# Pooling of the image tiles split between GpSimd and VectorE in a fused vision tower

## The chip, the cores and the metric

The kernel runs on one core of a Trainium2 chip. The metric is device time of one execution in microseconds; lower is better. The kernel before has a median of 2033.8 us over 3 runs (2013.52 to 2034.38).

## What is computed

The input is 64 images of 12 planes of 224 x 224 float32 (154 MB). The reference is a tower of three layers; cut to what matters here:

```python
# layer 1, for each image: sums over patches of 16 x 16 pixels, then a small product
pooled = x.reshape(B, 12, 14, 16, 14, 16).sum(axis=(3, 5))
h = einsum('bcij,ce->bije', pooled, channel_weights)      # 196 tokens of 192
# layer 2: h += softmax(Q K^T / sqrt(192)) V on the layernorm of h, one head
# layer 3 on the layernorm of h: a router takes the best 98 of 196 tokens for each of
#   4 experts (top_k of a softmax); fc1 with an MLP part (768) and q, k, v (12 heads of 16),
#   attention over 196 tokens, gelu, fc2, weighted by the gates, added to h
```

## The kernel before, in words

**Groups and bodies.** Images go in 8 groups of 8. While the third layer's attention and MLP of one group run, the pooling, the first attention and the routing of the next are done in between. The program is a prologue (pooling and routing of group 0 with nothing beside them, and pooling of the first half of group 1), a loop body that runs six times, a body behind it for the second last group, and a last body that has no next group. A body has 96 slots: 8 images by 12 heads. In each slot TensorE computes one head's scores twice (`peak`, whose row maxima VectorE takes, and `score`, whose exponentials ScalarE takes); the other work is placed at slot numbers. Behind the 96 slots the body has an opening, which computes the hidden layer of the next group.

**The order** on every engine is this one list, sorted by slot number; each engine walks through it and executes the entries that have a part for it, strictly in order. Engines wait for each other by semaphores alone. A slot number sets only what comes behind what; it is no time.

**Pooling.** A tile holds 8 planes: 112 partitions (8 planes x 14 rows of patches), each with 16 x 224 = 3584 floats, 1.6 MB. A group has 12 tiles, in 4 pairs of images (`m`) of 3 tiles (`t`). There are three tile buffers (`NX`). For a tile, in order: ScalarE's queue issues the load (`fetch`), VectorE sums the patches with seven `tensor_reduce`, each for two of the 14 patch columns (`pool`, L1211), GpSimd spreads the 14 sums over a masked square (`own_row`, L1457), TensorE adds the three tiles of a pair (`planes`, L734) and makes tokens of them (`tok`, L744). The semaphore `pooled` counts tiles that VectorE has summed; both `own_row` and the load of the tile three further on wait for it. In a loop body, tiles 6 to 11 of the next group are pooled from slot 0 on (`pace` 0.8: one `pool` every 0.8 slots), and tiles 0 to 5 of the group after it from slot 42 on (`pace` 1.25). The body behind the loop has the first six alone, the last body none.

**Routing** of the next group begins at slot 37 in a body: `norm1_scale` (VectorE sums, GpSimd raises to the power -0.5 in L1466, VectorE multiplies in L1243 and copies in L1247, TensorE transposes in L752), then 8 steps `first_max` and 8 steps `first_exp`, for each of which GpSimd makes a masked copy (`own_image`, L1486), then the gates (`gate_scale`, `gate_logits`, `gates`: two more powers on GpSimd, between them and behind them short VectorE instructions such as L1322 and L1328), then `choose`: 13 rounds on VectorE, each the eight largest of a row (L1342) and their replacement (L1347). Each round needs the one before. `chosen` (L834 on TensorE) waits for the last of them, `spread` (L1364, L1367) is behind it on VectorE, and the next group's `turn_u`, `project` and `hidden` on TensorE need `spread`.

**GpSimd** has, beside the masked copies, `own_row` and the powers, one addition per image to the result (`fc2`, L1494).

## Time and profile before

| | |
|---|---|
| runs | 2013.52, 2034.38, 2033.8 us; median 2033.8 |
| the profiled execution | 2031.33 us, its span 2029.5 us (1.8 us lie outside the span) |
| granted TensorE clock, mean | 0.861 of full speed |
| TensorE matmul busy | 1627.6 us, 80% |
| VectorE busy | 1226.3 us, 60% |
| ScalarE busy | 846.7 us, 42% |
| GpSimd busy | 248.4 us, 12% |

The page's line for an engine gives its busy time, the share of the span and the number of instructions. A group of instructions is one source line with one shape; "idle before" is how long the engine stood still just before them, and what it then waited for. TensorE is called PE, its weight loads PEld, VectorE DVE, ScalarE ACT, GpSimd POOL. Where a wait ends by "issue", the profile shows no releaser.

### The profile page before, as it was taken

The page shows a single profiled execution, that of the slowest core. Times are in us where ns is not written, and L with a number is a line of the kernel's source. Part 1 is how long each engine was busy: PE and PEld are TensorE (multiplying, and loading weights), DVE is VectorE, ACT ScalarE, POOL GpSimd, SP SyncE. Part 2 cuts the span into 40 slices and gives each one's busy share as a digit, 9 for nine tenths or more (in the row PEclk, how much of TensorE's full clock was granted, in tenths as well). Part 3 has the DMA queues.
Part 4 walks back from the last instruction along what each step waited for, and adds up shares of the span by engine and source line. Part 5 has one row for each costly group of instructions (what it writes and reads, how often), then busy time and mean ns, then how long its engine had stood idle before and what let it go on. Part 6 is the DMA issues. An engine that isn't in the chain of part 4 may idle for free.

```text
span 2029.5 us, 39123 instructions
## 1 busy us (share of the span) xinstructions
PE 1627.6 (80%) x12434; PEld 1306.0 (64%) x12434; DVE 1226.3 (60%) x2822; ACT 846.7 (42%) x1934; POOL 248.4 (12%) x318
## 2 busy tenths in 40 slices
PE   5116388968998788969799688987889698988998
PEld 2004366757676677758577576766667576767786
DVE  2465577673776557773776647664676747553453
ACT  1001154434444344435444344433544354544653
POOL 2002001110012001110011100210011100210000
PEclk8557599978799788978899789987899788998899
DMA  2993456433764437424655337534464335211220
GB/s 70 220 248 103 116 119 151 105 101 70 170 133 107 101 89 180 102 71 101 152 118 123 86 88 187 106 97 98 119 146 107 98 75 132 40 22 37 46 56 16
DMA packets 161085, 218.53 MB, mean 108 GB/s; under 512 B 135099, under 2 KB 149605, under 8 KB 150118
## 3 DMA queue, kind: packets, MB, share of 16 engines
q10 hardware_dynamic: 12288, 154.15, 28.8%
q1 hardware_dynamic: 148582, 61.68, 16.9%
q8 instruction: 115, 1.88, 0.4%
q14 instruction: 100, 0.82, 0.2%
HBM read 186.57 MB, written 28.90 MB: 106 GB/s over the span
## 4 chain that ended last, share of the span: by engine, by line
issue 47%; PE 30%; DMA 8%; DVE 6%; POOL 5%; ACT 2%; SPq 1%; POOLq 0%; ACTq 0%; DVEq 0%
PE bank L859 6%; PE bank L952 4%; DMA xt<-in_x_dram 4%; PE bank L869 3%; POOL var L1466 3%; PE bank L887 2%; DMA qs<-shiftT 2%; PE bank L921 2%; PE bank L783 2%; DVE psums L1211 2%; PE bank L794 2%; POOL fin L1494 1%; PE bank L906 1%; PE bank L767 1%; DVE peaks L1403 1%
## 5 line engine op out<-in xcount | busy, mean ns | idle before, releaser
L1403 DVE TENSOR_REDUCE peaks<-bank 98x2 f32<-98x392 f32 x768 | 427.2, 562 | 325.6 <-PE bank L887 312.9
L1099 ACT ACTIVATE Pb<-bank 98x392 f32<-98x392 f32 x768 | 375.1, 497 | 362.7 <-PE bank L906 314.1
L1211 DVE TENSOR_REDUCE psums<-xt 112x2 f32<-112x512 f32 x672 | 442.3, 679 | 82.3 <-DMA xt<-in_x_dram 51.6
L887 PE MATMUL bank<-ks,qs 96*98 96x196 f16 x1536 | 278.6, 270 | 91.3 <-DVE peaks L1403 46.4
L952 PE MATMUL bank<-w2T,hid 128*98 128x192 f32 x1536 | 309.0, 341 | 0.0
L887 PEld LDWEIGHTS bank<-ks,qs 96*98 96x98 f16 x1536 | 169.4, 132 | 197.0 <-issue 107.2
L906 PE MATMUL bank<-qs,ks 97*98 97x196 f16 x1536 | 279.5, 268 | 13.6 <-DMA qs<-shiftT 12.4
L952 PEld LDWEIGHTS bank<-w2T,hid 128*98 128x98 f32 x1536 | 245.8, 174 | 2.7
L906 PEld LDWEIGHTS bank<-qs,ks 97*98 97x98 f16 x1536 | 177.7, 137 | 28.3 <-DMA qs<-shiftT 13.8
L921 PE MATMUL bank<-Pb,vals 98*32 98x196 f32 x3072 | 190.9, 371 | 4.4 <-ACT Pb L1099 2.4
L1494 POOL TENSOR_TENSOR fin<-fin,both 98x384 f32<-98x384 f32 x64 | 64.0, 1000 | 790.1 <-DVE fin L1428 790.1
L1014 ACT COPY oT<-bank 128x196 f32<-128x196 f32 x192 | 61.9, 322 | 200.2 <-PE bank L921 189.6
L859 PE MATMUL bank<-UT,M 104*128 104x196 f32 x768 | 142.6, 337 | 0.0
L1457 POOL TENSOR_TENSOR spread_p<-psums,cst 112x196 f32<-112x196 f32 x96 | 50.0, 521 | 700.4 <-DVE psums L1211 700.4
L1392 DVE TENSOR_TENSOR qk<-bank,qk 96x392 f16<-96x392 f32 x128 | 71.9, 562 | 105.5 <-ACT qk L1086 101.9
L859 PEld LDWEIGHTS bank<-UT,M 104*128 104x128 f32 x768 | 131.7, 196 | 0.9 <-issue 0.2
L921 PEld LDWEIGHTS bank<-Pb,vals 98*32 98x32 f32 x3072 | 86.8, 117 | 70.5 <-issue 42.4
L1077 ACT ACTIVATE hid<-bank 128x392 f32<-128x392 f32 x192 | 94.1, 497 | 83.7 <-PE bank L859 83.5
L869 PE MATMUL bank<-UT,M 104*96 104x196 f32 x512 | 124.5, 398 | 0.1
L734 PE MATMUL bank<-spread_p,cst 112*24 112x196 f32 x192 | 43.3, 368 | 96.4 <-POOL spread_p L1457 96.3
L952 PE MATMUL bank<-w2T,onT 96*98 96x192 f32 (+1 forms) x512 | 108.6, 335 | 0.0
L869 PEld LDWEIGHTS bank<-UT,M 104*96 104x96 f32 x512 | 99.2, 204 | 11.7 <-issue 3.8
(181 smaller groups left out, 1834.3 us busy)
## 6 DMA issues: line engine op xcount, KB each, us to landing
xt<-in_x_dram ACTq DMA_DIRECT2D x96, 1568.0 KB, 9.0
qk_scratch<-qk SPq DMA_DIRECT2D x64, 294.0 KB, 3.7
qs<-qk_scratch SPq DMA_DIRECT2D x192, 73.5 KB, 3.3
ks<-qk_scratch SPq DMA_DIRECT2D x192, 73.5 KB, 3.6
out_dram<-fin SPq DMA_DIRECT2D x64, 147.0 KB
qs<-shiftT SPq DMA_DIRECT2D x128, 2.3 KB
hid<-in_L_ffn_w_dram SPq DMA_DIRECT2D x1, 1440.0 KB
hid<-in_L_ffn_w_dram SPq DMA_DIRECT2D x1, 960.0 KB
```

The source lines that it names most:

```text
L859: mm = pe.matmul(ps[:, T * j:T * j + T], M[:, 128 * f:128 * f + 128], UT[:, i, :], start=True, stop=True)
L869: mm = pe.matmul(ps[0:DC, T * c:T * c + T], M[:, f:f + DC], UT[:, i, :], start=True, stop=True)
L887: mm = pe.matmul(peak_ps[s][0:HT, T * q:T * q + T], qs[0:KS, i % NSTACK, h, HT * q:HT * q + HT], ks[0:KS, i % NSTACK, h, :], start=True, s ...
L906: mm = pe.matmul(score_ps[s][0:HT, T * k:T * k + T], ks[:, i % NSTACK, h, HT * k:HT * k + HT], qs[:, i % NSTACK, h, :], start=True, stop=True)
L921: mm = pe.matmul(ps[32 * j:32 * j + 32, 0:T], vals[:, i % 2, q, h, :], Pb[:, (H * i + h) % NP, q, :], start=(q == 0), stop=(q == 1))
L952: mm = pe.matmul(misc_ps[slot][0:HT, D * h:D * h + D], lhs, w2T[0:w, f, :], start=(f == 0), stop=(f == NF + 1))
L1077: act.activation(hid[:, i, 2 * b:2 * b + 2, :].rearrange("p a b -> p (a b)"), ps[:, 0:2 * T], ACT.Gelu).then_inc(free, 1)
L1099: act.activation(Pb[:, (H * i + h) % NP, :, :].rearrange("p a b -> p (a b)"), score_ps[s][0:HT, 0:2 * T], ACT.Exp, scale=float(DH) ** -0.5 ...
L1211: last = dve.tensor_reduce(psums[:, m % 2, t, 2 * p:2 * p + 2], v[:, 2 * p:2 * p + 2, :, :], AX.XY, ALU.add)
L1392: dve.tensor_tensor(qk16[:, m, 1, :, :].rearrange("p c t -> p (c t)"), misc_ps[slot][0:DC, 0:2 * T], qk16[:, m, 0, :, :].rearrange("p c t ...
L1403: dve.tensor_reduce(peaks[:, h // 6, :, h % 6], peak_ps[s][0:HT, 0:2 * T].rearrange("p (q k) -> p q k", q=2), AX.X, ALU.max, negate=True). ...
L1494: gp.tensor_tensor(fin[:, i % 2, :, :], fin[:, i % 2, :, :], resid[:, i % NRES, :, :], ALU.add) \
```

## The change

GpSimd adds the lower eight of the 16 pixel rows of every patch row onto the upper eight, in place in the tile buffer, in four instructions of 448 elements on each partition (`halve`). VectorE then sums what is left, 8 x 224 elements, in two instructions of seven patch columns each instead of seven of two. A new semaphore `halved` stands between them; the wait for the loaded tile moves from VectorE to GpSimd. The four `halve` take the slots of the first four old pieces; the two `pool` take the slots of the last two old pieces, plus 2. What hangs on the end of a tile (`own_row`, `fetch`, `planes`, `tok`) is moved by 2 slots with them. In the prologue the routing starts 3 slot numbers later; in the bodies `pace` for the first six tiles is 0.72 instead of 0.8, so that they end about where they did.

```diff
 PIECES = GRID // 2
+HALVES = 4
+SPLIT = 2
@@ pooling
         for p in range(PIECES):
             slot = start + pace * (PIECES * t + p)
-            ops.append((slot, ("pool", dg, m, t, p)))
+            if p < HALVES:
+                ops.append((slot, ("halve", dg, m, t, p)))
+            if p >= PIECES - SPLIT:
+                ops.append((slot + 2, ("pool", dg, m, t, p - PIECES + SPLIT)))
+        slot += 2
         ops.append((slot + 1, ("own_row", dg, m, t)))
@@ prologue
-    end = TILES * PIECES * GRP // PAIR + 3
+    end = TILES * PIECES * GRP // PAIR + 6
@@ body
-        pace = 0.8
+        pace = 0.72
@@ VectorE
                 if p == 0:
-                    dve.wait_ge(x_in[n_ % NX], 16 * (TILES * (GRP // PAIR) // NX * G_ + n_ // NX + 1))
+                    dve.wait_ge(halved, 12 * G_ + n_ + 1)
                     dve.wait_ge(masked, 4 * G_ + max(m - 1, 0))
-                v = xt[:, n_ % NX, :].rearrange("p (k j w) -> p j k w", k=PATCH, w=PATCH)
-                last = dve.tensor_reduce(psums[:, m % 2, t, 2 * p:2 * p + 2], v[:, 2 * p:2 * p + 2, :, :],
+                w = GRID // SPLIT
+                v = xt[:, n_ % NX, 0:XROW // 2].rearrange("p (k j w) -> p j k w", k=PATCH // 2, w=PATCH)
+                last = dve.tensor_reduce(psums[:, m % 2, t, w * p:w * p + w], v[:, w * p:w * p + w, :, :],
                                          AX.XY, ALU.add)
-                if p == PIECES - 1:
+                if p == SPLIT - 1:
                     last.then_inc(pooled, 1)
@@ GpSimd
+            def halve(at, G_, dg, m, t, p):
+                n_ = TILES * m + t
+                if p == 0:
+                    gp.wait_ge(x_in[n_ % NX], 16 * (TILES * (GRP // PAIR) // NX * G_ + n_ // NX + 1))
+                w = XROW // 2 // HALVES
+                top = xt[:, n_ % NX, w * p:w * p + w]
+                last = gp.tensor_tensor(top, top, xt[:, n_ % NX, XROW // 2 + w * p:XROW // 2 + w * p + w], ALU.add)
+                if p == HALVES - 1:
+                    last.then_inc(halved, 1)
```

**VectorE in the rounds of `choose`, loop body.** L1403 takes row maxima for the attention, L1342 with L1347 is a round, L1211 is a `pool`; REGISTER_ALU rows set up waits. Two rounds of the 13, before:

```order
L1403 TENSOR_REDUCE peaks<-bank 98x2
L1407 REGISTER_ALU
L1342 MAX top<-rows 32x8
L1198 REGISTER_ALU
L1347 MATCH_REPLACE rows<-top,rows 32x196
L1198 REGISTER_ALU
L1211 TENSOR_REDUCE psums<-xt 112x2
L1342 MAX top<-rows 32x8
L1198 REGISTER_ALU
L1347 MATCH_REPLACE rows<-top,rows 32x196
```

The same two rounds now (L1410, L1349 with L1354; a `pool` would be L1218):

```order
L1410 TENSOR_REDUCE peaks<-bank 98x2
L1414 REGISTER_ALU
L1349 MAX top<-rows 32x8
L1204 REGISTER_ALU
L1354 MATCH_REPLACE rows<-top,rows 32x196
L1204 REGISTER_ALU
L1349 MAX top<-rows 32x8
L1204 REGISTER_ALU
L1354 MATCH_REPLACE rows<-top,rows 32x196
```

Of the seven `pool` that stood from the copy of the rows up to the last round, one is left, in front of the first round; another now stands between the copy of the selection (`chosen`) and `spread`, where none was.

**GpSimd at the first power of the routing, loop body.** L1466 is the power, L1486 the masked copies of `own_image`, L1494 the addition of the results. Before:

```order
L1465 ISA
L1466 TENSOR_TENSOR var<-var,cst 98x16
L1480 ISA
L1486 TENSOR_SCALAR tm<-tT,cst 128x196 x2
L1492 REGISTER_ALU
```

Now (L1484 the power, L1478 the `halve`, L1475 its wait for the tile, L1504 the masked copies):

```order
L1483 ISA
L1484 TENSOR_TENSOR var<-var,cst 98x16
L1475 ISA
L1478 TENSOR_TENSOR xt<-xt 112x448 x2
L1498 ISA
L1504 TENSOR_SCALAR tm<-tT,cst 128x196 x2
```

Two additions of the next tile stand right behind the power, on whose result VectorE's multiplication waits. Behind the third power stand two `halve` as well, where before one `own_row` stood.

**VectorE behind slot 93 of a loop body.** L1428 is the multiplication of a result, which waits for TensorE's `fc2`; L1218 is the copy of `tok`. Before:

```order
L1211 TENSOR_REDUCE psums<-xt 112x2 x4
L1189 REGISTER_ALU
L1426 ISA
L1428 TENSOR_TENSOR fin<-bank,gate 98x192 x2
L1433 REGISTER_ALU
L1211 TENSOR_REDUCE psums<-xt 112x2
L1189 REGISTER_ALU
L1218 COPY tok_raw<-bank 98x96
```

Now (L1435 the multiplication, L1218 the `pool`, L1225 the copy of `tok`):

```order
L1399 TENSOR_TENSOR qk<-bank,qk 96x392
L1195 REGISTER_ALU
L1433 ISA
L1435 TENSOR_TENSOR fin<-bank,gate 98x192 x2
L1440 REGISTER_ALU
L1214 REGISTER_ALU
L1218 TENSOR_REDUCE psums<-xt 112x7 x2
L1195 REGISTER_ALU
L1225 COPY tok_raw<-bank 98x96
```

One short `pool` stood between the multiplication and the copy, now both long ones of the tile do; TensorE's `planes` for these tiles stands behind slot 95 in both.

## Rows read from the trace of the kernel before

**Rows 1.** The page: span, and busy time of three engines (share of span, instructions).

```profile
span 2029.5 us, 39123 instructions
...
PE 1627.6 (80%) x12434; PEld 1306.0 (64%) x12434; DVE 1226.3 (60%) x2822; ACT 846.7 (42%) x1934; POOL 248.4 (12%) x318
```

**Rows 2.** Groups by shape: count, busy us, mean ns, idle us before, what ended it.

```profile
L1211 DVE TENSOR_REDUCE psums<-xt 112x2 f32<-112x512 f32 x672 | 442.3, 679 | 82.3 <-DMA xt<-in_x_dram 51.6 <-DVE peaks L1403 11.1 <-DVE on_tok L1416 2.8
L1403 DVE TENSOR_REDUCE peaks<-bank 98x2 f32<-98x392 f32 x768 | 427.2, 562 | 325.6 <-PE bank L887 312.9 <-DVE on_tok L1416 1.5 <-DVE prob L1328 1.1
...
L1494 POOL TENSOR_TENSOR fin<-fin,both 98x384 f32<-98x384 f32 x64 | 64.0, 1000 | 790.1 <-DVE fin L1428 790.1
...
L1457 POOL TENSOR_TENSOR spread_p<-psums,cst 112x196 f32<-112x196 f32 x96 | 50.0, 521 | 700.4 <-DVE psums L1211 700.4
...
L1286 DVE TENSOR_REDUCE var<-tmp 98x8 f32<-98x200 f32 x16 | 5.8, 362 | 0.5
```

**Rows 3.** Engine busy time in three stretches of the third loop body.

```profile
core 0: us, PE busy (x) PEld busy (x) DVE busy (x) ACT busy (x) POOL busy (x), PEclk, DMA share, GB/s
733.20:798.90 65.70, 57.55 (x441) 45.13 (x440) 50.95 (x97) 31.85 (x73) 5.05 (x8) 0.82 0.69 163
798.90:876.00 77.10, 73.48 (x611) 58.23 (x610) 51.38 (x117) 37.23 (x88) 14.18 (x23) 1.00 0.51 111
876.00:929.20 53.20, 37.60 (x289) 29.60 (x288) 37.98 (x109) 17.97 (x44) 7.96 (x6) 0.74 0.35 90
```

**Rows 4.** The same three stretches of the body behind the loop.

```profile
1661.90:1728.00 66.10, 53.34 (x441) 42.02 (x439) 50.55 (x97) 32.95 (x75) 5.08 (x8) 0.87 0.50 113
1728.00:1803.00 75.00, 71.19 (x601) 57.48 (x601) 36.85 (x91) 36.58 (x85) 12.64 (x20) 1.00 0.21 36
1803.00:1851.10 48.10, 34.34 (x289) 28.09 (x288) 27.97 (x92) 18.54 (x45) 7.03 (x4) 0.82 0.10 21
```

**Rows 5.** Images 0 to 2 of the last body, which pools nothing.

```profile
1880.70:1933.80 53.10, 49.85 (x425) 40.92 (x424) 26.46 (x54) 31.70 (x72) 2.00 (x2) 0.87 0.25 47
```

**Rows 6.** Waits of TensorE: total us, times, longest us.

```profile
PE bank L834 <- issue: 51.7, 8, 18.2
```

**Rows 7.** VectorE by line, 888 to 912 us (`choose` of the third body).

```profile
L1211 DVE TENSOR_REDUCE psums<-xt 112x2 f32<-112x512 f32 x7 | 4.8, 683 | 0.4 <-DVE peaks L1403 0.2
```

**Rows 8.** VectorE by line, 208.8 to 227.6 us (`choose` of the prologue).

```profile
L1211 DVE TENSOR_REDUCE psums<-xt 112x2 f32<-112x512 f32 x9 | 6.2, 686 | 0.6
```

**Rows 9.** Timeline at the last tile of group 0: start us, us, instruction, idle before.

```profile
140.81 4.25 DVE L1211 TENSOR_REDUCE psums<-xt 112x2 f32<-112x512 f32 x7 [2.11 <-DMA xt<-in_x_dram]
```

**Rows 10.** Timeline at the gate's second power in the third body.

```profile
883.07 2.89 POOL L1466 TENSOR_TENSOR var<-var,cst 98x16 f32<-98x16 f32 x1 [1.67 <-DVE var L1316]
885.93 0.52 POOL L1457 TENSOR_TENSOR spread_p<-psums,cst 112x196 f32<-112x196 f32 x1
886.00 0.48 DVE L1322 TENSOR_TENSOR var<-var 98x16 f32<-98x16 f32 x1
```

**Rows 11.** Two lines' instructions, duration ns min/median/max.

```profile
L1322 DVE TENSOR_TENSOR var<-var x8: 175/480/482, 207.2 to 1813.0; 98x16 f32<-98x16 f32 x8
...
L1211 DVE TENSOR_REDUCE psums<-xt x672: 671/676/689, 65.3 to 1723.4; 112x2 f32<-112x512 f32 x168
```

**Rows 12.** Timeline at the first normalization of the third body.

```profile
809.01 0.36 DVE L1243 TENSOR_TENSOR a_tok<-z_tok,var 98x192 f32<-98x192 f32 x1 [1.23 <-POOL var L1466]
...
809.40 0.29 DVE L1247 COPY x_tok<-a_tok 98x256 f32<-98x256 f32 x1
...
809.75 0.39 PE L752 MATMUL bank<-cst,x_tok 98*128 98x98 f32 x2 [1.38 <-DVE x_tok L1247]
```

**Rows 13.** Timeline at the end of the third body's 96 slots.

```profile
929.10 0.69 DVE L1211 TENSOR_REDUCE psums<-xt 112x2 f32<-112x512 f32 x1
...
930.57 1.17 PE L734 MATMUL bank<-spread_p,cst 112*24 112x196 f32 x6 [1.10 <-POOL spread_p L1457]
```

**Rows 14.** DMA issues of x tiles: KB each, us to landing.

```profile
xt<-in_x_dram ACTq DMA_DIRECT2D x96, 1568.0 KB, 9.0
```

4 lines of the change are left out of this document (2 added, 2 removed).

## The prediction

> **What bounds the kernel now.** I began with the page [rows 1]: TensorE has matmuls running in 80% of the span, VectorE is at 60%, GpSimd at 12%. No engine is full, so the sum has to be made stage by stage. The groups [rows 2] say how large the object of the change is: 672 pooling instructions of 679 ns, 442.3 us of VectorE.
>
> Then I cut a loop body at the first `score` of an image. The third one runs from 733.2 to 966.6 us (233.4 us), in three stretches and an opening [rows 3]: images 0 to 2 take 65.7 us with VectorE busy for 50.95, images 3 to 5 take 77.1 with TensorE busy for 73.48 and VectorE for 51.38, images 6 and 7 take 53.2 with TensorE at only 37.60 and VectorE at 37.98. So TensorE sets the pace in the middle, and at both ends it is VectorE's order that holds it up. Two comparisons show how much. The last body pools nothing, and its images 0 to 2 take 53.1 us instead of 65.7 [rows 3, 5]; of these 12.6 I give some 6 to TensorE's own `planes` and `tok`, an estimate (TensorE is busy for 57.55 instead of 49.85 there, not all of it work), so that about 6.4 are the most that 42 `pool` on VectorE cost. The body behind the loop pools in images 0 to 2 as the loop does (66.1 us), but not from slot 42 on: its images 3 to 5 take 75.0 instead of 77.1, its images 6 and 7 48.1 instead of 53.2 [rows 3, 4]. The largest single wait is at the end of `choose`: TensorE stands at L834 for 51.7 us in 8 times [rows 6], since the 13 rounds on VectorE are late.
>
> **The price of the pieces.** A `tensor_reduce` of 200 elements takes 362 ns, of 512 elements 679 [rows 2], so 1.02 ns an element; the new one has 896, which makes 679 + 384 x 1.02 = 1.07 us. Seven of the old ones take 4.25 us in a row [rows 9], that is 0.61 each, because the next starts before the last has ended; the new one then occupies 1.00. VectorE has 4.25 us a tile now and 2.0 after the change. GpSimd's additions: 196 elements take 521 ns, 384 take 1000 [rows 2], 2.55 ns an element; 448 make 1.16 us, 4.65 a tile (at least 4.0 by the 384-element row as it stands, at most 4.8 in proportion to the 196-element one). With `own_row` GpSimd has 5.2 us a tile.
>
> **Is this covered?** In images 0 to 2 a slot lasts 65.7/36 = 1.83 us, a tile comes every 5.04 slots = 9.2 us. The first `pool` of a tile stands 3.4 slots = 6.3 us behind its last `halve`, and the load of a tile stands 6.8 slots = 12.4 us in front of its first `halve`, against 9.0 us to landing [rows 14]. GpSimd only waits behind `own_row`, which stands behind the next tile's halves. I cost the additions themselves at nothing in the bodies; if this cover were gone, VectorE would wait, and the row maxima behind it, and TensorE with them.
>
> **Loop body, term by term.**
> Images 0 to 2: 42 x 0.61 = 25.5 us of `pool` become 12. The bound is 6.4 us for all of it; a queue shortens most by what is taken first, so for half of it I take 4.5 (bounds 1.5 and 6.4).
> Images 3 to 5: 24 `pool` (14.5 us) cost 2.1 us at most, 75.0 against 77.1; six remain of 1.00. I take 8.5/14.5 of it, -1.2 (0 to -2.1).
> `choose`: between 888 and 912 us seven `pool` stand in VectorE's list [rows 7] while TensorE waits, 7 x 0.61 = 4.2 us; one of 1.00 is left, which makes -3.2. A new one in front of `spread` costs up to 1.0, of which I charge half, as TensorE has other work there: -2.7 (-2.0 to -5.1, the whole difference of images 6 and 7).
> First power: in the trace, when GpSimd goes from the power at once to another instruction that reads SBUF (521 ns), VectorE's 16-element instruction that waited for the same power takes 480 ns where it takes 175 alone; it ends when GpSimd's ends [rows 10, 11]. That is the median of eight. Pooling instructions, with GpSimd beside them or not, stay within 671 and 689 ns [rows 11]. The Trainium skill's page "SBUF — State Buffer", section "Who interferes with whom", gives the reason: VectorE's second pair of SBUF ports is also GpSimd's, held for a whole instruction, needed by a VectorE instruction with two SBUF inputs and never by `tensor_reduce`; the rows agree in both. In the changed order two additions stand right behind the power, and VectorE's multiplication of `norm1` (L1243, 0.36 us, two SBUF inputs) meets the first. It ends some 0.95 us later (1.16 in place of 0.52, and what the 305 ns of the row then become). TensorE waits at L752 for the copy behind it already, for 1.38 us [rows 12], so this is on the path. Of the copy itself no row shows whether the second addition holds it up; bounds 0 and 0.95, I take 0.5, halfway, since neither row is nearer. Together +1.45. The same section says that a float32 copy within SBUF needs the pair too; by it the term would be +1.9.
> Third power: L1322 meets a 1.16 us addition instead of the 0.52 us `own_row`, +0.64, and L1328 the tail of the next, +0.1: +0.75 (0.6 to 1.0).
> End of the body: TensorE waits for 1.10 us at `planes` for the last `own_row`, behind one `pool` at 929.10 [rows 13]. Now both long ones stand there, behind the same multiplication: 2.0 for 0.61, +1.4.
> Sum: -4.5 - 1.2 - 2.7 + 1.45 + 0.75 + 1.4 = -4.8 us a body, six times: -28.8.
> The body behind the loop has only the first term: -4.5.
>
> **Prologue.** Its first 12 tiles come at the pace of the loads (VectorE waits 2.11 us for the twelfth, [rows 9]). Two tiles are still being loaded while one is worked on, so a tile that is held for 7 instead of 4.3 us leaves the loads going. But the last one is 4.65 + 2.07 us from landing to sum instead of 4.25: +2.5. Then `choose`, where nothing hides VectorE: nine `pool` [rows 8], eight in front of the end of the last round, become two: 8 x 0.61 - 2.0 = -2.9, the ninth -0.3; two more in front of the second power -1.2; behind `spread` 2.0 for three short ones, +0.15; the third power +0.75. Sum -0.9 (-4 to +2).
>
> **The forecast** is -28.8 - 4.5 - 0.9 = -34 us against the profiled execution's own 2031.3 us (span 2029.5 and 1.8 outside): **1997 us**. That execution is 2.5 us under the median of the runs, 2033.8.
>
> **Rivals.**
> (a) *VectorE's load was mostly hidden, and the new waits eat the rest.* For it: TensorE is at 80%, and the row maxima have two banks. Against it: VectorE has 78% in images 0 to 2. With the low ends of the gains and the high ends of the costs a body gets -1.5 - 0 - 2.0 + 1.9 + 1.0 + 1.4 = +0.8, six of them +4.8, the body behind them -1.5: **2035 us**.
> (b) *The relief passes through whole.* TensorE's granted clock is 0.74 of full speed in images 6 and 7, where it waits most, 0.82 in images 0 to 2 and 1.00 in images 3 to 5, where it is busy [rows 3]; fewer waits may bring back some of it, and the comparison bodies contain that effect. With the high ends, -6.4 - 2.1 - 5.1 + 0.95 + 0.7 + 1.4 = -10.5 a body, six times -63, then -6.4 and -3: **1958 us**.
> (c) *The halves come too late (the slower side).* VectorE's `pool` waits in order for `halved`, and behind it stand the row maxima that TensorE needs. The place is images 0 to 2, where a tile has 9.2 us and the way from `fetch` to the first `pool` is longest. There are 78 tiles in the bodies. If each `pool` stood for one addition, 1.16 us, that would be +90: **2087 us**. It decides from 0.45 us a tile, where the gain is gone, and the kernel is over 1% slower from 0.7. For it: GpSimd's list is in order, and a tile's last two halves may stand behind `own_row` or a result's addition that waits for VectorE. Against it: the 6.3 us computed above.
> That the new instructions do not relieve VectorE at all is excluded by the slope of its own rows: half the elements in two instructions.
>
> **Chances.** The forecast's case 0.46, (a) 0.27, (b) 0.16, (c) 0.11. What a measurement here can tell from no change is about 1%, 20 us. Faster by more than that: the forecast's case nearly whole (0.42), (b) 0.16, and 0.02 of (a), 0.60; slower: (c), 0.11; within 1%: 0.29. The range of 8 in 10 reaches halfway into (b) and just over (a): 1964 to 2037 us.
>
> **What would show it.** `pool` as 192 instructions of 1.07 us, `halve` as 384 of 1.16, VectorE's busy time lower by some 240 us, GpSimd's at some 690. TensorE's wait at L834 smaller by about 3 us a body; its wait behind the first power larger by 1 to 2, and the multiplication of `norm1` near 1.3 us long instead of 0.36; `planes` at a body's end waited for 2.5 us. A body of 228 to 229 us. No waits of `pool` for `xt` from GpSimd outside the prologue; if VectorE's idle time names `halve` as its releaser by more than some 0.5 us a tile, (c) holds and I was wrong on the cover. If the bodies' images 0 to 2 stay at 65 us with VectorE well under 70%, (a) does.

## The result, and the profile after

The change made the kernel slower: 2079.05 us (median of 4 runs, 2071.04 to 2083.39) against 2034.09 us of the kernel before in the same session, ratio 1.0251 with an interval of 1.0167 to 1.0335. The forecast was 1997 us, and 2079 lies outside its range. The profiled execution has a span of 2078.0 us, 48.5 more than before.

The page's lines that answer to [rows 1], and the groups that answer to [rows 2] (count, busy us, mean ns, idle us before and what ended it):

```profile
span 2078.0 us, 39086 instructions
...
PE 1639.6 (79%) x12434; PEld 1318.0 (63%) x12434; DVE 1071.0 (52%) x2342; ACT 846.7 (41%) x1934; POOL 668.8 (32%) x702
...
L1410 DVE TENSOR_REDUCE peaks<-bank 98x2 f32<-98x392 f32 x768 | 425.1, 565 | 445.1 <-PE bank L893 422.4 <-DVE on_tok L1423 4.4 <-DVE peaks L1410 3.2
...
L1478 POOL TENSOR_TENSOR xt<-xt 112x448 f32<-112x448 f32 x384 | 426.3, 1133 | 107.8 <-DMA xt<-in_x_dram 107.7
...
L1218 DVE TENSOR_REDUCE psums<-xt 112x7 f32<-112x896 f32 x192 | 206.0, 1082 | 90.6 <-POOL xt L1478 67.5 <-DVE on_tok L1423 8.7 <-DVE peaks L1410 5.3
```

The relief is there: an addition takes 1133 ns (forecast 1160), a `pool` 1082 (1070), GpSimd is busy for 668.8 us (690), and the pooling on VectorE costs 206.0 us instead of 442.3. But VectorE's busy time fell by 155 us and not by 240. Some 49 us of the difference are durations of instructions that do the work of before and now take longer; the rest is bookkeeping (records of neighbouring instructions overlap, busy time counts them once, and there are 480 fewer of them). The longer durations are the first trace of what went wrong.

By the first `score` of each body, the 48.5 us lie here: the prologue 273.4 us instead of 266.5, the six loop bodies 236.2 to 245.3, together 1438.8 instead of 1395.4 (a mean of 239.8 against 232.6, +7.2 each), the body behind them 220.9 instead of 218.8, the last 144.9 instead of 148.8. (The last body takes 144.5 to 145.4 or 148.7 to 148.8 in all kernels of this study, changed or not; that difference is not the change's.) So the question is the loop body: -4.8 us was forecast, +7.2 came.

The third body runs from 752.2 to 991.0 us now. Its three stretches, in the columns of [rows 3]:

```profile
752.20:817.80 65.60, 54.43 (x444) 42.26 (x442) 38.58 (x68) 32.22 (x73) 22.65 (x24) 0.89 0.79 171
817.80:897.40 79.60, 73.78 (x602) 58.73 (x601) 45.44 (x100) 36.58 (x86) 30.92 (x39) 0.98 0.40 93
897.40:949.60 52.20, 38.18 (x294) 30.39 (x292) 32.64 (x93) 18.29 (x46) 17.62 (x15) 0.77 0.37 97
```

Images 0 to 2 take 65.6 us as before (65.7), although VectorE is busy for 12.4 us less there; images 3 to 5 take 2.5 us more; images 6 and 7 take 1.0 less; the rest, behind 949.6, takes 41.4 instead of 37.4. Image by image, image 3 is 2.4 us longer and the last one with the opening 2.9, image 0 is 3.1 shorter and image 1 2.5 longer.

**Image 3: the first power.** Timeline of the changed kernel (start us, us, instruction, idle before), the place of [rows 12]:

```profile
824.45 2.90 POOL L1484 TENSOR_TENSOR var<-var,cst 98x16 f32<-98x16 f32 x1 [9.51 <-DVE var L1245]
...
827.32 2.33 POOL L1478 TENSOR_TENSOR xt<-xt 112x448 f32<-112x448 f32 x2
827.39 1.28 DVE L1250 TENSOR_TENSOR a_tok<-z_tok,var 98x192 f32<-98x192 f32 x1 [1.23 <-POOL var L1484]
...
828.70 1.10 DVE L1254 COPY x_tok<-a_tok 98x256 f32<-98x256 f32 x1
...
829.86 0.39 PE L758 MATMUL bank<-cst,x_tok 98*128 98x98 f32 x2 [3.11 <-DVE x_tok L1254]
```

The multiplication takes 1.28 us instead of 0.36 and the copy 1.10 instead of 0.29. Each ends with one of GpSimd's two additions. TensorE waits for 3.11 us instead of 1.38, +1.73.

**Image 6: the third power**, the same view:

```profile
906.08 2.21 POOL L1478 TENSOR_TENSOR xt<-xt 112x448 f32<-112x448 f32 x2
906.15 1.09 DVE L1329 TENSOR_TENSOR var<-var 98x16 f32<-98x16 f32 x1 [0.23 <-POOL var L1484]
907.27 1.05 DVE L1330 TENSOR_SCALAR var<-var 98x16 f32<-98x16 f32 x1
...
909.32 0.33 PE L832 MATMUL bank<-cst,prob 98*32 98x98 f32 x2 [3.80 <-DVEq L1336]
```

The instruction behind the met one, a TENSOR_SCALAR on 16 elements with a single input, is held for the whole second addition (it takes 0.17 us alone). TensorE's wait is 3.80 us. The same wait in the kernel before and, ahead of the experiments, in relief_alone, which has the changed order and no additions, each in the third body:

```profile
887.69 0.49 PE L826 MATMUL bank<-cst,prob 98*32 98x98 f32 x2 [1.15 <-DVEq L1329]
```

```profile
872.23 0.33 PE L832 MATMUL bank<-cst,prob 98*32 98x98 f32 x2 [2.02 <-DVEq L1336]
```

So of the 2.65 us between 1.15 and 3.80 only 1.78 are the meeting; 0.87 come with the changed order alone.

**The opening: gate8**, which the prediction doesn't speak of. GpSimd's list has nothing between the last result's addition and the next body's first tile, so it runs eight additions in a row right behind that addition, since the tiles are loaded by then:

```profile
977.59 8.75 POOL L1478 TENSOR_TENSOR xt<-xt 112x448 f32<-112x448 f32 x8
...
979.05 0.85 DVE L1385 TENSOR_TENSOR cg<-sel,prob 98x64 f32<-98x64 f32 x1
...
979.93 1.03 DVE L1386 COPY gate<-cg 98x64 f32<-98x64 f32 x1
...
983.17 1.05 DVE L1390 TENSOR_TENSOR gate<-cg,gate 98x16 f32<-98x16 f32 x1
...
984.96 1.03 PE L893 MATMUL bank<-ks,qs 96*98 96x196 f16 x4 [2.19 <-DVE peaks L1410]
...
985.79 4.18 PE L865 MATMUL bank<-UT,M 104*128 104x196 f32 x12
```

Five instructions that the kernel before does in 0.19 to 0.21 us each take 5.0 us together, each to the end of one addition. The row maxima stand behind them, TensorE waits for 2.19 us, and twelve matmuls that took 2.15 us a few us earlier take 4.18. The granted clock tells why. Busy time by stretch, in the opening of the changed kernel and then in the same part of the opening before (the clock is the third number from the end):

```profile
968.20:984.90 16.70, 14.57 (x97) 14.10 (x95) 9.25 (x15) 7.77 (x16) 8.27 (x8) 1.00 0.13 19
984.90:991.00 6.10, 5.68 (x20) 4.86 (x21) 1.52 (x4) 1.68 (x4) 1.44 (x2) 0.51 0.02 5
```

```profile
944.60:961.30 16.70, 16.70 (x114) 16.49 (x113) 5.98 (x17) 7.73 (x17) 1.00 (x1) 1.00 0.13 19
```

Up to 984.9 us TensorE has the full clock (1.00, that is 2.4 GHz); behind its wait it has 0.51 (1.2 GHz). Before, it was busy through the whole stretch and kept it. The last 6.1 us of the first five loop bodies say the same: the clock there is 0.50 or 0.51 in four of them in the changed kernel (1.00 in the fourth body, behind a wait as long) and 0.96 to 1.00 before.

**Image 1: the load of ks.** DMA issues and TensorE's wait, first in the kernel before, then in the changed one (SPq and ACTq are the queues that issue):

```profile
764.81 0.30 SPq L636 DMA_DIRECT2D qs<-qk_scratch  x1
...
765.50 0.32 ACTq L993 DMA_DIRECT2D xt<-in_x_dram  x1
...
776.83 0.56 PE L887 MATMUL bank<-ks,qs 96*98 96x196 f16 x2 [2.89 <-DMA ks<-qk_scratch]
```

```profile
780.91 0.32 ACTq L999 DMA_DIRECT2D xt<-in_x_dram  x1
783.17 0.30 SPq L642 DMA_DIRECT2D qs<-qk_scratch  x1
...
795.21 0.56 PE L893 MATMUL bank<-ks,qs 96*98 96x196 f16 x2 [5.86 <-DMA ks<-qk_scratch]
```

Since VectorE is through with a tile earlier, the next x load is issued 2.3 us in front of the small loads of q and k, not 0.7 behind the first of them. The six loads of 73.5 KB behind it take 7.9 to 9.3 us to land; in the kernel before the first two took 2.6 and 4.1, the other four 8.9 to 9.4. The 3.1 us that image 0 gained are spent in this wait, 5.86 us instead of 2.89, and the pattern is in every loop body: 3.9 to 6.6 us at image 1, before 2.9 to 3.6. Over the whole execution, in the view of [rows 6] (total us, times, longest):

```profile
PE bank L893 <- DMA ks<-qk_scratch: 49.9, 13, 6.6
...
PE bank L840 <- issue: 44.6, 8, 16.9
PE bank L832 <- DVEq L1336: 35.3, 8, 10.4
PE bank L758 <- DVE x_tok L1254: 25.9, 8, 5.8
```

Before, they were 28.5 us (ks), 51.7 ([rows 6]), 20.4 and 15.5.

**The body's end**, the place of [rows 13]:

```profile
949.58 2.08 DVE L1218 TENSOR_REDUCE psums<-xt 112x7 f32<-112x896 f32 x2 [0.29 <-DVE fin L1435]
...
952.31 1.18 PE L740 MATMUL bank<-spread_p,cst 112*24 112x196 f32 x6 [2.52 <-POOL spread_p L1464]
```

### The profile page after: what moved, and what is told of

Same layout as the page of the kernel before. It is cut to its first block, busy times and chain, and to the rows that moved or that the text cites. A ratio compares the mean times of both kernels' runs of the same rounds, so it can differ in the third digit from the quotient of the medians.

```text
span 2078.0 us, 39086 instructions
## 1 busy us (share of the span) xinstructions
PE 1639.6 (79%) x12434; PEld 1318.0 (63%) x12434; DVE 1071.0 (52%) x2342; ACT 846.7 (41%) x1934; POOL 668.8 (32%) x702
## 3 DMA queue, kind: packets, MB, share of 16 engines
q10 hardware_dynamic: 12288, 154.15, 28.5%
## 4 chain that ended last, share of the span: by engine, by line
issue 36%; PE 33%; POOL 14%; DMA 7%; DVE 7%; ACT 2%; SPq 1%; POOLq 0%; ACTq 0%; DVEq 0%
POOL xt L1478 8%; PE bank L958 5%; PE bank L865 5%; POOL var L1484 3%; DMA xt<-in_x_dram 3%; PE bank L893 3%; PE bank L875 3%; PE bank L927 3%; PE bank L789 2%; PE bank L912 2%; PE bank L773 2%; POOL fin L1512 2%; PE bank L800 2%; DMA ks<-qk_scratch 1%; DVE peaks L1410 1%
## 5 line engine op out<-in xcount | busy, mean ns | idle before, releaser
L1410 DVE TENSOR_REDUCE peaks<-bank 98x2 f32<-98x392 f32 x768 | 425.1, 565 | 445.1 <-PE bank L893 422.4
L1478 POOL TENSOR_TENSOR xt<-xt 112x448 f32<-112x448 f32 x384 | 426.3, 1133 | 107.8 <-DMA xt<-in_x_dram 107.7
L893 PE MATMUL bank<-ks,qs 96*98 96x196 f16 x1536 | 278.5, 270 | 103.0 <-DMA ks<-qk_scratch 49.9
L1218 DVE TENSOR_REDUCE psums<-xt 112x7 f32<-112x896 f32 x192 | 206.0, 1082 | 90.6 <-POOL xt L1478 67.5
L865 PE MATMUL bank<-UT,M 104*128 104x196 f32 x768 | 153.2, 354 | 0.0
L865 PEld LDWEIGHTS bank<-UT,M 104*128 104x128 f32 x768 | 142.3, 208 | 0.5 <-issue 0.2
L875 PE MATMUL bank<-UT,M 104*96 104x196 f32 x512 | 132.2, 417 | 0.1
## 6 DMA issues: line engine op xcount, KB each, us to landing
qs<-qk_scratch SPq DMA_DIRECT2D x192, 73.5 KB, 3.3
ks<-qk_scratch SPq DMA_DIRECT2D x192, 73.5 KB, 3.6
```

Source lines behind the costliest of these rows:

```text
L865: mm = pe.matmul(ps[:, T * j:T * j + T], M[:, 128 * f:128 * f + 128], UT[:, i, :], start=True, stop=True)
L875: mm = pe.matmul(ps[0:DC, T * c:T * c + T], M[:, f:f + DC], UT[:, i, :], start=True, stop=True)
L893: mm = pe.matmul(peak_ps[s][0:HT, T * q:T * q + T], qs[0:KS, i % NSTACK, h, HT * q:HT * q + HT], ks[0:KS, i % NSTACK, h, :], start=True, s ...
L1218: last = dve.tensor_reduce(psums[:, m % 2, t, w * p:w * p + w], v[:, w * p:w * p + w, :, :], AX.XY, ALU.add)
L1410: dve.tensor_reduce(peaks[:, h // 6, :, h % 6], peak_ps[s][0:HT, 0:2 * T].rearrange("p (q k) -> p q k", q=2), AX.X, ALU.max, negate=True). ...
L1478: last = gp.tensor_tensor(top, top, xt[:, n_ % NX, XROW // 2 + w * p:XROW // 2 + w * p + w], ALU.add)
```

## The experiments

Each ratio is to the kernel before, run in the same session on the same chip (its medians were 2023.85 to 2035.48 us). "Body" is the mean of the six loop bodies in the profiled execution, "prologue" the time of the first `score`; the kernel before has 232.6 and 266.5, the changed one 239.8 and 273.4. Body and prologue are those of one execution, which can lie off the median of its kernel: that of hold_fetch is the fastest of its ten, 15 us under their median, and that of best the slowest of its five, 13 us over it.

| kernel | median us | ratio (interval) | body | prologue |
|---|---|---|---|---|
| relief_alone | 2008.71 | 0.9841 (0.9795 to 0.9887) | 229.5 | 260.2 |
| adds_alone | 2084.35 | 1.0237 (1.0184 to 1.0289) | 240.6 | 269.9 |
| adds_hold | 2034.45 | 1.0050 (1.0027 to 1.0072) | 232.4 | 270.1 |
| hold | 2021.96 | 0.9922 (0.9890 to 0.9954) | 230.2 | 269.0 |
| hold_oldpro | 2019.09 | 0.9915 (0.9879 to 0.9951) | 230.2 | 271.3 |
| hold_gate8 | 2047.65 | 1.0110 (1.0065 to 1.0155) | 234.8 | 269.7 |
| hold_np | 2034.17 | 1.0056 (1.0023 to 1.0089) | 231.8 | 268.5 |
| halves8 | 2038.65 | 1.0056 (1.0023 to 1.0090) | 232.9 | 270.7 |
| hold_fetch | 2028.41 | 1.0001 (0.9976 to 1.0025) | 229.3 | 269.7 |
| relief_halfload | 1908.27 | 0.9443 (0.9411 to 0.9475) | 222.8 | 212.3 |
| hold_pace | 2047.43 | 1.0113 (1.0074 to 1.0152) | 234.9 | 266.9 |
| best | 2052.81 | 1.0137 (1.0103 to 1.0171) | 236.9 | 272.9 |
| hold_x2 | 1998.73 | 0.9863 (0.9810 to 0.9916) | 228.5 | 260.7 |
| hold_x4 | 2014.74 | 0.9939 (0.9914 to 0.9964) | 232.2 | 261.3 |
| before_x2 | 2016.61 | 0.9953 (0.9927 to 0.9979) | 231.9 | 259.9 |
| after_x2 | 2059.21 | 1.0171 (1.0115 to 1.0226) | 238.6 | 258.2 |

Where in the body it lies, as means over the six loop bodies (us):

| kernel | images 0 to 2 | images 3 to 5 | images 6 and 7 with the opening |
|---|---|---|---|
| before | 65.9 | 77.1 | 89.6 |
| changed | 67.1 | 80.0 | 92.7 |
| relief_alone | 65.9 | 75.9 | 87.6 |
| hold | 66.1 | 76.3 | 87.9 |
| relief_halfload | 58.9 | 75.9 | 88.1 |

### The two halves of the change apart

relief_alone, from the changed kernel; the lower eight rows are left out of the sums:

```diff
-                    dve.wait_ge(halved, 12 * G_ + n_ + 1)
+                    dve.wait_ge(x_in[n_ % NX], 16 * (TILES * (GRP // PAIR) // NX * G_ + n_ // NX + 1))
-            run(gp, {"halve": halve, "own_row": own_row, "norm1_scale": norm1_scale, "gate_scale": gate_scale,
+            run(gp, {"own_row": own_row, "norm1_scale": norm1_scale, "gate_scale": gate_scale,
```

> The changed kernel without GpSimd's additions: VectorE sums the upper eight pixel rows alone (the lower eight are left out of the result), waiting for the load itself as before. It keeps the changed order. Theory 1 (VectorE's relief is real, and the additions on GpSimd cost more than it through the SBUF ports and through the longer hold of a tile): the first score of the first body at 262 to 266 us, a body at 226 to 229 us instead of 238.8, in all 1995 to 2010 us. The multiplication of norm1 is back at 0.36 us and the five instructions of gate8 at 0.2. Theory 2 (the relief is lost anyway, because images 0 and 1 then wait for the load of ks and qs, and TensorE is the bound elsewhere): a body at 232 to 236, images 0 and 1 together still at 43 us with a wait of TensorE of 5 to 6 us on ks, in all 2030 to 2050.

adds_alone, from the kernel before; the results of the additions are used by nobody:

```diff
+            def halve(at, G_, dg, m, t, p):
...
+                gp.tensor_tensor(spare[:, p % 2, :], cst[0:PP, 0:w], cst[0:PP, w - 200:2 * w - 200], ALU.add)
```

> The kernel before, pooling as before on VectorE, with four GpSimd additions of 448 elements a tile beside it, which read the constants and write a spare tile, and whose results nobody needs. They stand in GpSimd's list where the changed kernel has them. Theory 1 (ports): the short VectorE instructions with SBUF operands that meet an addition take about 1.1 us each, gate8 costs 3 to 4 us a body, norm1 1.7, the gate 2 to 3; a body goes from 233.4 to 240 to 244 us, in all 2075 to 2100. The prologue's tiles keep their pace (the first score at 267 to 270 us). Rival (the additions are harmless, the harm is in the split itself: longer reduces, the wait for halved, the moved slots): a body within 1 us of 233.4, in all 2030 to 2040.

The relief alone gives 1.6%, the additions alone cost 2.4%. The additions that nobody waits for cost a body 8.0 us, more than the whole change does. In their trace VectorE's two instructions of `norm1` are as long as in the changed kernel, as means over eight executions of which six are met:

```profile
L1247 DVE TENSOR_TENSOR a_tok<-z_tok,var 98x192 f32<-98x192 f32 x8 | 8.4, 1045 | 11.7 <-POOL var L1480 11.7
L1251 DVE COPY x_tok<-a_tok 98x256 f32<-98x256 f32 x8 | 7.2, 899 | 0.3
```

So it is not the data, nor the wait for `halved`, nor the buffers: it is what GpSimd does at that moment. (The places are not quite the same. Four of the five `gate8` instructions are held, not all five; behind the third power it is the TENSOR_SCALAR (L1323 of before) and `prob`, but not the multiplication; and at the end of `choose` a TENSOR_SCALAR takes 824 ns instead of 250 and two of the four instructions of `spread` 1.40 and 1.52 us instead of 0.58. The 8.0 us are therefore no sum of the changed kernel's places.) The second thing to see is in the relief alone. Its bodies are 3.1 us shorter than before, where the forecast had 8.4 for its three gains less 1.4 for the body's end, 7.0, and TensorE waits for ks for 59.4 us in all instead of 28.5. By the table, images 3 to 5 give the forecast's 1.2 us there, and images 0 to 2 nothing. That loss has nothing to do with GpSimd (adds_alone waits for ks for 26.0 us). The time is in the first theory's range, the body and the first score just beside theirs (226 to 229 and 262 to 266 expected); the second theory's wait for ks, 5 to 6 us at image 1, is there as well.

### Keeping the additions off three places

hold, from the changed kernel. The additions for the next body's first tile wait until `gate8` is done; those behind the first and third power wait for the copy of `norm1` and for `prob`. No addition is removed.

```diff
@@ VectorE, behind the last gate8 instruction
+                dve.sem_inc(gate8_done, 1)
@@ halve
+                if dg == 1 and (m, t, p) == (AHEAD, 0, 0):
+                    gp.wait_ge(gate8_done, G_)
+                if dg == 2 and (m, t, p) == (0, 0, 0):
+                    gp.wait_ge(a_ready, G_)
+                if dg == 2 and (m, t, p) == (1, 1, 0):
+                    gp.wait_ge(prob_ready, G_)
```

> The changed kernel with GpSimd held back at three places by waits in front of a tile's first addition: the eight additions at a body's start wait until gate8 is through on VectorE, the two behind the first power until norm1's copy is through, the two behind the third power until the gates' probabilities are. Nothing else changes. Theory 1 (these three meetings are most of the loss in the bodies): gate8 0.2 us an instruction, norm1's multiplication 0.36; a body at 231 to 233 us instead of 238.8, in all 2030 to 2042. Rival (the meetings lie beside other work of TensorE; the loss is in the DMA wait of image 1 and in the clock): a body at 236 to 239, in all 2065 to 2080. Rival 2 (the held additions come late for pool): VectorE waits for the additions in the bodies, and a body is over 240.

Three waits take 9.6 us off a body and turn 1.0251 into 0.9922. The opening's timeline in the kernel with holds:

```profile
954.64 0.21 DVE L1386 TENSOR_TENSOR cg<-sel,prob 98x64 f32<-98x64 f32 x1
...
955.57 0.19 DVE L1391 TENSOR_TENSOR gate<-cg,gate 98x16 f32<-98x16 f32 x1
955.96 8.74 POOL L1486 TENSOR_TENSOR xt<-xt 112x448 f32<-112x448 f32 x8 [2.74 <-DVEq L1392]
```

The same eight additions start 2.7 us later and meet nothing. As means over six bodies, images 3 and 6 take 21.7 and 20.6 us, 3.7 and 2.7 less than in the changed kernel. The kernel came out under the first theory's range (2030 to 2042).

hold_gate8 has the first of the three waits alone:

```diff
-                if dg == 2 and (m, t, p) == (0, 0, 0):
-                    gp.wait_ge(a_ready, G_)
-                if dg == 2 and (m, t, p) == (1, 1, 0):
-                    gp.wait_ge(prob_ready, G_)
```

> The changed kernel with the gate8 hold alone: in each opening GpSimd's additions for the next body's first tile wait until VectorE's five short gate8 instructions are done; the additions behind the first and third power stay where the change put them. Theory P (places add up): by the images of the third body, image 7 with the opening and image 0 take back 2.4 + 1.7 us, the rest nothing, so about -4.1 us for each of 6 or 7 openings: 2052 us, gate8's instructions 0.2 us again, a_tok still 1.28 us and the third power's multiplication still 1.09. Rival Q (one clock effect, and the places are not independent: the first hold that gives TensorE its clock back gives most of it): 2030 to 2040. Rival R (gate8 is off the path): 2075 to 2083.

hold_np has the other two:

```diff
-                if dg == 1 and (m, t, p) == (AHEAD, 0, 0):
-                    gp.wait_ge(gate8_done, G_)
```

> The changed kernel with the two holds of the routing alone: the additions behind the first power wait for the multiplication and copy of norm1, those behind the third power for prob; gate8 stays as in the changed kernel, met by the additions. Theory P: image 3 gets 3.3 us shorter and image 6 3.6 us, six times: about -40 us, 2039 us, with gate8's instructions still near 1 us. Rival Q (not independent): within 8 us of the full hold's 2022. Rival R (the wait for the power only moves the additions, which then meet later instructions): over 2055.

Theory P holds: 2.51 points over the kernel before become 1.10 with the one and 0.56 with the others, gains of 1.4 and 2.0 that add up to 3.4; all three gave 3.3. By the traces' bodies they are not quite independent (5.0 and 8.0 against 9.6). The clock follows the places: in the last 6.1 us of the first five loop bodies it is 0.91 to 0.98 in hold_gate8 and 0.50 to 0.53 in hold_np, where TensorE waits 2.17 to 2.19 us at `gate8` in each.

halves8 has eight additions of 224 elements a tile, nothing held:

```diff
-HALVES = 4
+HALVES = 8
-            if p < HALVES:
-                ops.append((slot, ("halve", dg, m, t, p)))
+            if p < HALVES // 2:
+                ops.append((slot, ("halve", dg, m, t, 2 * p)))
+                ops.append((slot, ("halve", dg, m, t, 2 * p + 1)))
```

> The changed kernel with eight additions of 224 elements a tile instead of four of 448, nothing held. Theory P (a VectorE instruction that needs the shared ports waits for the end of the GpSimd addition that runs, whatever follows): an addition takes 0.58 us, and each of the met instructions (a_tok, x_tok, the third power's two, gate8's five) 0.5 to 0.7 us instead of 1.05 to 1.28; half of the 57 us that holding gave back, 2050 us. Rival S (the instruction waits until GpSimd stops, or for a fixed time): met instructions stay at 1.0 to 1.3 us and the time at 2079. Rival T (384 more instructions cost GpSimd their start-up and the halves come late): above 2079.

```profile
L1251 DVE TENSOR_TENSOR a_tok<-z_tok,var 98x192 f32<-98x192 f32 x8 | 5.5, 693 | 11.7 <-POOL var L1485 11.7
...
L1479 POOL TENSOR_TENSOR xt<-xt 112x224 f32<-112x224 f32 x768 | 480.5, 657 | 91.2 <-DMA xt<-in_x_dram 91.1
```

The multiplication of `norm1` takes 693 ns in the mean instead of 1046, and gate8's five, where they are met, 0.51 to 0.58 us instead of 0.85 to 1.05: a met instruction waits for the end of the addition that runs, so half the length costs about half. The ratio fell by 2.0 points, of the 3.3 that the holds gave. The smaller additions cost GpSimd 54 us more in all (657 ns and not 567), which nobody waits for. Rivals S and T are out.

adds_hold is adds_alone with the same three holds:

```diff
+                if dg == 1 and (m, t, p) == (AHEAD, 0, 0):
+                    gp.wait_ge(gate8_done, G_)
...
```

> The kernel before with four additions of constants a tile on GpSimd (the additions alone, ratio 1.0237), and the same three holds. Theory P (the additions cost only by what they meet at the three places): bodies again 233 us, a_tok 0.36 us, gate8 0.2 us, ratio 1.000 to 1.004, the rest in the prologue, which has no hold and took 3.4 us longer. Rival L (the additions' whole load on SBUF, or on the clock, costs as well): bodies 236 or more, ratio over 1.010.

The body is 232.4 us, the kernel before's 232.6: 384 additions, 429 us of GpSimd, cost a body nothing in all once they are off the three places. That is a balance, not the absence of meetings: the three instructions at `choose` and `spread` are still held in each of the six bodies, as long as in adds_alone. The ratio of 1.005 lies just above what theory P gave; the prologue, where nothing is held, took 270.1 us.

### Where the gain of images 0 to 2 went

relief_halfload is the relief alone with the upper eight rows of a tile loaded and no more (the lower ones are missing in its result, as in relief_alone):

```diff
-                act.dma_start(xt[:, t % NX, :],
+                act.dma_start(xt[:, t % NX, 0:XROW // 2],
-                              [bass.ds(first_plane * GRID, PP), :]).then_inc(x_in[t % NX], 16)
+                              [bass.ds(first_plane * GRID, PP), 0:XROW // 2]).then_inc(x_in[t % NX], 16)
```

> The relief alone (VectorE sums the upper eight rows, GpSimd adds nothing), and only the upper eight rows of each tile are loaded, 0.8 MB instead of 1.6; the lower rows are left out of the result, as in the relief alone. With full loads its bodies took 228.0 to 233.6 us and TensorE waited 59.4 us for ks in all, in the bodies' images 0 to 2. Theory D (what the pooling gives back in images 0 to 2 is lost again since the q and k loads meet an x load): the waits for ks fall under 10 us in all, a body takes 224 to 226 us, that is the 4.5 us of the forecast; with the prologue's loads twice as fast (some -25 us) about 1950 us. Rival E (TensorE has no more to gain in images 0 to 2 and waits for VectorE's row maxima instead): bodies stay at 229 to 230, about 1982 us.

```profile
PE bank L893 <- DMA ks<-qk_scratch: 1.3, 3, 0.6
```

The waits for ks are gone and the body takes 222.8 us, 6.7 less than with full loads. All of it is in images 0 to 2, 58.9 us instead of 65.9, where those waits were. Theory D holds and E falls; of the 6.7 us, some may be what half the bytes give beside these waits. (Most of the 100 us against relief_alone is the prologue, 47.9 us shorter, since its pace is that of the loads, and the bodies' 40.)

hold_fetch has the holds, and issues two of the x loads three slots later:

```diff
+LATE = {(1, 2, 2): 3, (1, 3, 1): 3}
-            ops.append((slot + 2, ("fetch", dg, m, t)))
+            ops.append((slot + 2 + LATE.get((dg, m, t), 0), ("fetch", dg, m, t)))
```

> The kernel with all three holds (2022 us), and two of the six loads that a body issues before its routing (the third and the fifth) issued 3 slots later, behind the q and k loads that they run into. In the hold kernel those small loads take 7 to 9 us instead of 3, and TensorE waits for ks 5.8 us at image 1. Theory D (what the pooling saved in images 0 to 2 went into this wait): the wait falls to under 3 us, image 1 from 26 to about 23 us, -3 us in 7 bodies: about 2000 us. Rival E (TensorE then waits for VectorE or for the third load elsewhere, the stretch being full): 2015 to 2025. Rival F (the later loads come too late for their halves, and VectorE's pool waits for halved in the bodies): above 2030.

A miss. The waits for ks fell from 59.2 to 37.1 us, but a single one of 10.8 us appeared (the second body's image 2 takes 31.9 us), and the ratio shows no gain. There two x loads, 1.8 us apart, meet the next set of q and k loads, of which three take 14.3 to 16.1 us to land. Its body mean is 0.9 us under that of hold, but the profiled execution is the fastest of ten; the ratio goes by all ten and is 0.8 points above that of hold, so a gain is not shown.

hold_x2 and hold_x4 leave the time of the loads alone and cut each into two or four DMAs, issued one behind the other (hold_x2 shown):

```diff
-                act.dma_start(xt[:, t % NX, :],
-                              x.rearrange("b c (i k) w -> (b c i) (k w)", k=PATCH)
-                              [bass.ds(first_plane * GRID, PP), :]).then_inc(x_in[t % NX], 16)
+                w = XROW // 2
+                for part in range(2):
+                    act.dma_start(xt[:, t % NX, w * part:w * part + w],
+                                  x.rearrange("b c (i k) w -> (b c i) (k w)", k=PATCH)
+                                  [bass.ds(first_plane * GRID, PP), w * part:w * part + w]) \
+                        .then_inc(x_in[t % NX], 16)
@@ halve
-                    gp.wait_ge(x_in[n_ % NX], 16 * (TILES * (GRP // PAIR) // NX * G_ + n_ // NX + 1))
+                    gp.wait_ge(x_in[n_ % NX], 32 * (TILES * (GRP // PAIR) // NX * G_ + n_ // NX + 1))
```

> The kernel with three holds (ratio 0.992; TensorE waits 59.2 us for ks in 15 times), each x tile loaded by two DMAs of 784 KB instead of one of 1568 KB, issued one behind the other. Theory D1 (a small q or k load waits behind the x load's large packets, 12.5 KB each; halved packets let it pass sooner): the waits for ks fall to about 40 us, 2 us less a body, ratio about 0.985. Rival D2 (what counts is the bytes in flight, whatever the packets): waits for ks 55 to 65 us, ratio 0.992 or, with ScalarE 0.36 us longer at each load, 0.992 to 0.998.

> The same with four DMAs of 392 KB a tile. Theory D1: the waits for ks fall under 30 us, 4 us less a body, less what three more DMA issues a tile take from ScalarE (1.1 us a tile, beside other work): ratio 0.978 to 0.985, bodies 225 to 228 us. Rival D2: waits for ks stay at 55 to 65 us and ScalarE's issues cost: ratio 0.995 to 1.005.

The queue's line on the page (packets, MB, share) and TensorE's waits, for hold, hold_x2 and hold_x4 in this order:

```profile
q10 hardware_dynamic: 12288, 154.15, 29.5%
...
PE bank L894 <- DMA ks<-qk_scratch: 59.2, 15, 6.8
```

```profile
q10 hardware_dynamic: 24576, 154.15, 30.2%
...
PE bank L894 <- DMA ks<-qk_scratch: 38.7, 11, 6.3
```

```profile
q10 hardware_dynamic: 49152, 154.17, 29.5%
...
PE bank L894 <- DMA ks<-qk_scratch: 18.9, 8, 4.1
...
PE bank L937 <- ACT oT L1024: 16.1, 29, 1.6
```

The bytes are the same, the packets 12.5, 6.3 and 3.1 KB, and the waits fall with them, as D1 says. These are single executions, and 12.6 of hold_x2's 20.5 us are waits at image 0, which come in some bodies and not in others; at image 1 the sum fell from 37.8 to 31.7 and, with four DMAs, to 11.7 us. The last is the clear step. The Trainium skill's page "DMA: Bandwidth & Descriptors", section "Queues, rings and completion order", says that an engine goes round its queues a packet at a time; these three runs agree. Four DMAs overdo it: ScalarE issues them at mostly 0.32 us each between its own instructions, TensorE waits for its copy `oT` for 16.1 us instead of 5.6, and the body is back at 232.2 us, outside what D1 expected.

The controls, with the same edit on the kernel before and on the changed one:

```diff
@@ load_tile, both
+                for part in range(2):
...
@@ VectorE, before_x2 (GpSimd in after_x2)
-                    dve.wait_ge(x_in[n_ % NX], 16 * (TILES * (GRP // PAIR) // NX * G_ + n_ // NX + 1))
+                    dve.wait_ge(x_in[n_ % NX], 32 * (TILES * (GRP // PAIR) // NX * G_ + n_ // NX + 1))
```

> The kernel before with each x tile loaded by two DMAs of 784 KB, nothing else: the control for hold_x2 (ratio 0.986). Theory: the smaller packets spare the kernel before part of its 28.5 us of ks waits (to about 18) and some us of the prologue: ratio 0.990 to 0.997, and hold_x2 stays 0.5 to 1% under it; that would be what the split of the pooling is worth once its meetings are gone. Rival: the two DMAs give all of it, ratio 0.986, and the split of the pooling is worth nothing even with the holds.

> The changed kernel (ratio 1.0251) with two DMAs a tile and no hold. Theory (the two causes are independent): the two DMAs give what they gave to the kernel with holds, 0.6 points, and up to 0.3 of the prologue: ratio 1.016 to 1.020. Rival: without the waits for ks the meetings at the ports cost less or more, ratio under 1.010 or still 1.025.

Both ratios came out as the first theory had it, but the waits for ks did not. They fell from 28.5 to 22.5 us in the kernel before (18 expected), and in the changed kernel they are 49.9 us with one DMA a tile and with two. So that packets of half the size spare TensorE its waits is shown with the holds alone, and clearly with four DMAs only. Much of what two DMAs give lies elsewhere. Of the 20.8 us by which after_x2's profiled execution is shorter than the changed kernel's, 15.2 are the prologue; of before_x2's 17.0 it is 6.6 (and 4.3 the loop bodies), of hold_x2's 18.6 against hold it is 8.3 (and 10.3 the bodies). In the prologue the twelfth tile has landed at 127.9 to 133.5 us in all four kernels that load a tile in two or four DMAs, and at 138.1 to 147.5 in all thirteen that load the whole tile in one.

Two DMAs give the kernel before 0.5 points and the changed one 0.8. hold_x2, at 0.9863, beats both kernels, and it is 0.9 points under before_x2: that, some 18 us, is what splitting the pooling is worth here when it meets nothing. The two intervals do not overlap (0.9916 and 0.9927), if barely.

### The prologue and the body's end

hold_oldpro is hold with group 0 pooled as before (`whole`: seven pieces a tile, VectorE alone), hold_pace moves the last tile of a body forward, and the third kernel, best, is hold_pace with both groups of the prologue pooled as before.

```diff
@@ hold_oldpro
-        front += pooling(0, m, TILES * PIECES * m, 1)
+        front += pooling(0, m, TILES * PIECES * m, 1, whole=True)
@@ hold_pace
-            front += pooling(2, m, 42 + 1.25 * TILES * PIECES * m, 1.25)
+            front += pooling(2, m, 42 + 1.22 * TILES * PIECES * m, 1.22)
@@ the third kernel: hold_pace, and
-        front += pooling(1, m, end + 10 + TILES * PIECES * m, 1)
+        front += pooling(1, m, end + 10 + TILES * PIECES * m, 1, whole=True)
```

> As the kernel with the three holds, and group 0 pooled as before (VectorE alone, seven reduces a tile), since nothing runs beside it. Theory (in the prologue a tile is held 7 us instead of 4.3, which leaves fewer loads under way and slows them, and the last one is longer): the first score 6 to 7 us earlier than in the kernel with the holds, at 265 to 268 us, the last tile's sums at 145 us instead of 152. Rival (the prologue's loss comes in the routing, by own_image behind the additions and the ports): only 0 to 3 us earlier.

> The kernel with three holds (ratio 0.992 to the kernel before), and the first six tiles of the group after next pooled with 1.22 instead of 1.25 slots a piece, so that the last tile's two pool and its own_row stand one or two slots in front of the body's end. Theory P (TensorE's wait at planes, 2.5 us, is the two long pool and nothing else): it falls to 0 to 1 us, a body 1.3 us shorter, 6 bodies: -8 us, ratio 0.988. Rival G (the two pool only move in front of another instruction that TensorE waits for, in choose or at prob): no change, 0.992.

> hold_pace, and both groups of the prologue pooled by VectorE alone in seven pieces a tile, as in the kernel before; the loop keeps the split. The prologue with the split took 268.5 to 273.4 us to the first score of the first body in six traces, before 266.5. Theory: -3 to -4 us against hold_pace, ratio 0.985 to 0.987. Rival: the prologue is set by the loads, whose pace differs from run to run by 4 us, and nothing changes: the ratio of hold_pace.

Taken whole, the prologue settles nothing. The split prologue took 266.9 to 273.4 us in seven traces, the old one 266.5 before and 272.9 in the third kernel here; what differs is the pace of the loads (the twelfth tile lands at 141.1 us in hold and at 145.1 in the changed kernel, by the same code, and at 140.8 to 147.5 with the old pooling). Counted from that landing to the first score the traces do part: 125.4 to 126.4 us with group 0 pooled as before (before, hold_oldpro, best, before_x2), 127.7 to 130.3 with the split (ten traces, those with two and four DMAs among them), 128.6 and 129.7 with the additions beside the old pooling (adds_alone, adds_hold), 118.1 with the relief alone. So the split costs the prologue some 2 to 4 us: the additions, which are held nowhere there, cost more than the relief gives. A kernel that holds them there too was not run. hold_oldpro is not faster than hold, since its tiles landed later.

hold_pace is a clear miss. TensorE's wait at `planes` falls from 2.52 to 1.38 us (0 to 1 expected), but other waits grow. TensorE in `choose` and at `spread`, of hold and then of hold_pace, both in the fourth body (the other bodies are alike):

```profile
1135.31 0.34 PE L841 MATMUL bank<-cst,rows 32*98 32x32 f32 x2 [3.96 <-issue]
...
1140.06 0.87 PE L849 MATMUL bank<-cst,both 98*104 98x98 f32 x4 [0.47 <-DVE both L1375]
```

```profile
1144.84 0.34 PE L841 MATMUL bank<-cst,rows 32*98 32x32 f32 x2 [5.03 <-issue]
...
1151.52 0.87 PE L849 MATMUL bank<-cst,both 98*104 98x98 f32 x4 [2.39 <-DVE both L1375]
```

That is 3.0 us lost for 1.1 gained, and images 0 and 3 are 1.4 and 1.0 us longer on the mean. It is rival G, at a price that rival G did not have; where the rest of the 4.6 us a body comes from was not traced.

## Why the prediction failed

The forecast's sum for a body was -4.5 - 1.2 - 2.7 + 1.45 + 0.75 + 1.4 = -4.8 us. By stretches, as means over the six bodies, it was -4.5 for images 0 to 2, +0.25 for images 3 to 5 and -0.55 for the rest; measured were +1.2, +2.9 and +3.2. Its terms, against the third body where nothing else is said:

- **Durations and the cover of the additions** were right (1133 and 1082 ns). Rival (c) did not come: VectorE waits for a halved tile 67.5 us in all, in 11 times, ten of them in the prologue and one of 0.7 us in the first body.
- **Images 0 to 2, -4.5: failed, -0.1 in the third body and +1.2 in the mean of six; with the relief alone 0.0.** "A queue shortens most by what is taken first" is true of VectorE, and image 0 shows it with 3.1 us; I did not ask what a tile that is done earlier triggers. Its successor's load starts earlier, and runs into the q and k loads (shown: with half the bytes the waits are gone and these images take 58.9 us instead of 65.9). This is rival (a)'s "the new waits eat the rest", but the new wait is that of a DMA, which rival (a) did not name.
- **Images 3 to 5, -1.2: right, but hidden.** In the changed kernel images 4 and 5 take as long as before, 54.6 us against 54.4, and only image 3 changed, for the worse. In relief_alone the three take 75.9 us instead of 77.1, the forecast's 1.2 to the tenth, and that exact is luck.
- **`choose`, -2.7: right in size.** TensorE's wait for the last round fell by 1.0 us in each loop body, not by the 3 that I had named as the sign; the rest is its wait for the row maxima ahead. In the third body the two waits at `choose` (VectorE's `peaks` ahead and the rounds) fell from 10.8 to 8.3 us, and TensorE waits for 0.4 us at `spread`, where it did not wait before.
- **First power, +1.45: its wait +1.73.** I took 0.5 us for the copy, halfway between 0 and 0.95; it was 0.81. The Trainium skill's page "SBUF — State Buffer", section "Who interferes with whom", lists `copy` among the operations that can take the shared pair; the trace agrees for this one (1.10 us instead of 0.29). The sum by it, +1.9, was the better one.
- **Third power, +0.75: its wait +2.65, of which the meeting is +1.78.** The failing words are "L1328 the tail of the next". Between the multiplication and `prob` stands L1323 (L1330 now), with one input, which the term left out. Two additions in a row catch two instructions in a row, and TENSOR_SCALAR from SBUF to SBUF is caught as the multiplication is (1.05 us instead of 0.17). The other 0.87 us are there with no addition at all (relief_alone 2.02, hold 2.01); why the order costs them stays open.
- **End of the body, +1.4: right** (1.10 to 2.52 us).
- **The body behind the loop, -4.5: +2.1.** Its images 0 to 2 wait for ks as the loop's do. The prologue's terms add up to -1.0 and not to -0.9, which changes nothing.
- **The opening: missing from the sum.** I looked for what the additions meet where the listing puts them behind a power, and not where GpSimd's list is empty and it runs ahead. There, eight additions meet the five instructions of `gate8` in each body. Removing that meeting alone gave 1.4 points of the ratio, some 29 us, out of the 82 by which I was off.

Two steps failed, then: the gain of images 0 to 2 (-4.5, came out at +1.2), which was sized without what a freed buffer starts, and the list of meetings, which lacked `gate8` (put at nothing, some 29 us in all) and L1323.

One thing runs through the three meetings: the price of one is not only its wait. Behind the wait of 2.19 us at `gate8` TensorE runs at a granted clock of 0.51, and holding that place alone took 5.0 us off the mean body; the holds together take 9.6 us off a body whose three meetings had, by their waits, some 5.7 (1.73, 1.78 and 2.19). Image 3 shows it too, in the means over six bodies: its clock is 1.00 before, 0.91 in the changed kernel and 1.00 in hold, and the hold gives it 3.7 us for a wait of 1.73. The rows of before had shown neither two held instructions in a row nor this; GpSimd was busy for 12% of the span there.

In the whole: forecast -34 us, measured +45 (medians). The holds account for some 67 us of ratio (1.0251 to 0.9922), the two DMAs for 0.6 points more (0.9922 to 0.9863), of which the kernel before has 0.5 too. Of the prologue's +6.9 us, 4.3 are the later landing of its twelfth tile, which the same code did not show in hold, and 2.6 come behind it. What stays open: why hold_fetch did not gain in its median, why a load in two DMAs lands the prologue's tiles earlier, and how much of the 7.0 us that half the bytes gave images 0 to 2 (65.9 to 58.9) could be had with whole loads.

## What to carry to other kernels

Work that an idle GpSimd takes over is free only where VectorE runs nothing of the kinds listed below at that time, so list every stretch in which GpSimd can run ahead of the order, the quiet ones too, and look there for short chains of VectorE on SBUF that TensorE waits for. Three waits that hold GpSimd back behind such chains gave 3.3% here, and no body paid for them. And when a buffer comes free earlier, look at what its next load will run into. The same load in two DMAs is worth a trial: it gave 0.5 to 0.8% in three kernels here, much of it in the prologue, where the tiles landed earlier.

## What the hardware showed

- Beside additions of 448 float32 elements that follow one another on GpSimd, these VectorE instructions lasted 0.85 to 1.28 us instead of 0.17 to 0.36, to the end of the addition that ran, and the next of them was caught again by the next addition: TENSOR_TENSOR with both inputs in SBUF (16 to 192 elements; in adds_alone also 416, 1.40 to 1.52 us instead of 0.58), TENSOR_SCALAR of 16 and COPY of 64 and 256 elements, both from SBUF to SBUF. With additions of 224 elements the short ones lasted 0.51 to 0.58 us.
- Not held beside the same additions, in the changed kernel: TENSOR_REDUCE from SBUF and PSUM (33 `pool` 1078 ns in the median against 1085 elsewhere, 173 row maxima 568 against 568), MAX8 (24, 344 ns), MATCH_REPLACE8 (16, 334 ns, as elsewhere, though it reads and writes SBUF), and copies and TENSOR_TENSOR with an input in PSUM (98x192: 357 ns in both). In adds_alone seven RECIPROCAL from SBUF to SBUF took 253 ns, as alone.
- A held instruction counts as busy: VectorE's busy share does not show that it stands still.
- A load of 73.5 KB took 3.3 us in the median and 4.2 at most when no x load was under way in the changed kernel; of the 200 that overlapped with a 1.6 MB load in packets of 12.5 KB on another queue, 119 took 7.0 to 10.3 us. With the holds, the waits that came of it fell from 59.2 to 38.7 and 18.9 us with packets of 6.3 and 3.1 KB; without them they stayed at 49.9 us with 6.3 KB.
- The prologue's twelve tiles of 1.6 MB had landed at 127.9 to 133.5 us when each came in two or four DMAs (four kernels), and at 138.1 to 147.5 when each came in one (thirteen kernels).
